# Ten of a step's 36 expert products set among the recurrent gates' products, in the last stage of a two-layer network

## The reference, cut to what matters

```python
def _L1_cond2_ref(video, seq, W_z, U_z, C_z, b_z, W_r, U_r, C_r, b_r, W, U, C, b):
    ...
    def step(h, xs):
        xzt, xrt, xht = xs
        z = jax.nn.sigmoid(xzt + h @ U_z + vz)
        r = jax.nn.sigmoid(xrt + h @ U_r + vr)
        hh = jnp.tanh(xht + r * h @ U + vh)
        h_new = (1.0 - z) * h + z * hh
        return (h_new, h_new)
    ...
def _L1_ffn_ref(x, Wg, routing_bias, W1, W2, W3, Ws1, Ws2, Ws3):
    E, K = (8, 4)
    ...
    h1 = jnp.einsum('bsd,ehd->ebsh', x, W1)
    h2 = jnp.einsum('bsd,ehd->ebsh', x, W2)
    eo = jnp.einsum('ebsh,edh->ebsd', jax.nn.sigmoid(h1) * h1 * h2, W3)
    out = out + jnp.einsum('ebsd,bse->bsd', eo, weights)
    return out
...
x = x + _L1_ffn_ref(_L1_cond2_ref(cond_1024, x, ...), ...)
```

## Time and profile before

| what | value |
|---|---|
| median of 3 runs | 2695.06 us |
| profiled execution, its own time | 2692.25 us |
| span of that execution | 2689.3 us |
| PE busy | 2413.2 us (90%) |
| DVE busy | 1898.1 us (71%) |
| ACT busy | 1206.2 us (45%) |
| steps of chunk 0 (no experts) | from 1573 to 1631 us of the span |
| the 240 steps with both | from 1631 to 2632 us |
| experts of the last chunk alone | from 2632 us to the end |

### The profile page before, as it was taken

How to read it: one execution, slowest core, us unless ns; L and a number is a source line. 1 busy time by engine, 2 the same in 40 slices (tenths; PEclk the granted TensorE clock), 3 DMA queues, 4 the chain that set the end, 5 groups by cost and what they waited for, 6 DMA issues and landing times. The chain is left out here.

```text
span 2689.3 us, 114287 instructions
## 1 busy us (share of the span) xinstructions
PE 2413.2 (90%) x47776; PEld 1955.5 (73%) x47776; DVE 1898.1 (71%) x7976; ACT 1206.2 (45%) x3950; POOL 163.7 (6%) x157
## 2 busy tenths in 40 slices
PE   3778999999999999987758858999999999999999
PEld 2555677777777777754436647888888888888888
DVE  4757777777777777788665666666666666666665
ACT  3225555555555555566436743333333333333333
POOL 0000000000000000000009900000000000000000
PEclk8668999999999999999858968999999999999999
DMA  6000000000000000011003330000000000000000
GB/s 186 2 2 3 5 5 5 5 5 5 5 5 5 6 5 3 5 44 30 4 1 119 95 99 22 9 9 9 9 9 9 9 9 9 9 9 9 5 5 6
DMA packets 53178, 53.35 MB, mean 20 GB/s; under 512 B 25126, under 2 KB 47288, under 8 KB 50746
## 3 DMA queue, kind: packets, MB, share of 16 engines
q1 hardware_dynamic: 47878, 30.57, 4.2%
q0 software_dynamic: 1728, 12.58, 1.4%
q10 hardware_dynamic: 3060, 2.90, 0.4%
HBM read 39.46 MB, written 6.57 MB: 17 GB/s over the span
## 5 line engine op out<-in xcount | busy, mean ns | idle before, releaser
L105 PE MATMUL p<-xn,m_h 128*128 128x128 f16 x6144 | 557.3, 219 | 0.0
L105 PE MATMUL p<-xn,m_l 128*128 128x128 f16 x3072 | 528.6, 219 | 0.0
L105 PEld LDWEIGHTS p<-xn,m_h 128*128 128x128 f16 x6144 | 479.8, 98 | 1.8
L607 PE MATMUL lg_b<-xn,lh 128*32 128x256 f16 x6144 | 300.2, 291 | 77.4 <-DVE lh L1089 69.3
L867 ACT ACTIVATE gl<-gt 128x128 f32<-128x128 f32 x324 | 100.2, 309 | 597.9 <-DVE gt L1065 597.4
L1065 DVE STREAM_TRANSPOSE gt<-lg_b 128x512 f32<-128x512 f32 x324 | 230.0, 710 | 180.5 <-PE lg_b L607 179.9
L882 ACT ACTIVATE hm<-xy,b 128x512 f32<-128x512 f32 x512 | 347.9, 680 | 0.0
L105 PEld LDWEIGHTS p<-xn,m_l 128*128 128x128 f16 x3072 | 300.6, 98 | 0.7
L2038 PE MATMUL po<-m_h,xn 128*128 128x256 f16 x1536 | 292.4, 272 | 2.2 <-DVE xn L2185 1.7
L607 PEld LDWEIGHTS lg_b<-xn,lh 128*32 128x32 f16 x6144 | 159.9, 101 | 161.5 <-DVE lh L1089 117.6
L607 PE MATMUL lg_b<-e_wh_hi,lh 128*32 128x256 f16 x4096 | 209.7, 282 | 30.5 <-DVE lh L1089 29.8
(11 more groups left out here) (400 smaller groups left out, 5975.6 us busy)
## 6 DMA issues: line engine op xcount, KB each, us to landing
m_stage<-in_m_w POOLq DMA_DIRECT2D x12, 1024.0 KB, 5.3
hs<-in_m_w SPq DMA_DIRECT2D x16, 384.0 KB, 3.3
x_dram<-x SPq DMA_DIRECT2D x16, 128.0 KB, 2.1
xs<-in_l_wv SPq DMA_DIRECT2D x1, 2048.0 KB
attention_dram<-att SPq DMA_DIRECT2D x16, 128.0 KB, 3.0
xn<-x_dram SPq DMA_DIRECT2D x16, 128.0 KB, 2.5
xn<-attention_dram SPq DMA_DIRECT2D x128, 16.0 KB, 1.8
out_dram<-xn SPq DMA_DIRECT2D x16, 128.0 KB, 2.2
```

The source lines that it names most:

```text
L105: ins = pe.matmul(out, w[wp](k), x[xp](k), start=start, stop=last and k == KT - 1 and xp == 1, skip_group_check=True)
L607: last = pe.matmul(gate_block(ae, j, par), lh[:, part, ae, k, u, :], columns(w[name], k, j), start=False, stop=(part == 1 and k == KT - 1) ...
```

## The change

TensorE's program of the last stage is put in another order; the instructions are the same. `zr_gates` is cut into `zr_low_weights` and `zr_high_weights`. `hidden` takes a range of its 36 products. In a step with recurrence and experts the first 4 (none in slot 0) stand between the two halves of the gates' products, 26 (30 in slot 0) where all stood, and the last 6 behind the candidate's products, ahead of `down`. The wait for `a_done` stays at the first hidden product, and `hid_pe` is raised by the last one.

```diff
+        HIDDEN, BEFORE, AFTER = 2 * GM * KT * 3, 4, 6
...
-            def zr_gates(i, slot):
+            def zr_low_weights(i, slot):
...
+
+            def zr_high_weights(i, slot):
+                n = i * C + slot
+                par, r = state_at(i, slot)
                 if n > 0:
                     pe.wait_ge(h_lo, n)
...
-            def hidden(i, slot):
+            def hidden(i, slot, lo, hi):
+
                 n = group(i, slot, 0)
-                if n is None:
+                if n is None or lo == hi:
                     return
                 par = (i - 1) % 2
-                if slot == 0:
-                    pe.wait_ge(h_lo, i * C)
-                if n >= 2:
-                    pe.wait_ge(a_done, n - 1)
-                for mat, bank in enumerate((p1[n % 2], p2[n % 2])):
...
+                if lo == 0:
+                    if slot == 0:
+                        pe.wait_ge(h_lo, i * C)
+                    if n >= 2:
+                        pe.wait_ge(a_done, n - 1)
+                banks = p1[n % 2], p2[n % 2]
+                for q in range(lo, hi):
+                    mat, j, k, term = q // 18, q // 6 % GM, q // 3 % KT, q % 3
+                    w, g = (m12_h, m12_l, m12_h)[term], (g_hh, g_hh, g_hl)[term]
+                    last = pe.matmul(banks[mat][:, j * CW:(j + 1) * CW], w[:, mat, k, GM * slot + j, :], g[:, par, k, :],
+                                     start=(q % 18 == 0), stop=(q % 6 == 5), skip_group_check=True)
+                if hi == HIDDEN:
+                    last.then_inc(hid_pe, 1)
...
             for i, slot in steps():
+                before, after = (BEFORE if slot else 0, AFTER) if scans(i) else (0, 0)
                 if scans(i):
-                    zr_gates(i, slot)
+                    zr_low_weights(i, slot)
+                    hidden(i, slot, 0, before)
+                    zr_high_weights(i, slot)
...
-                hidden(i, slot)
+                hidden(i, slot, before, HIDDEN - after)
                 if scans(i):
                     candidate(i, slot)
+                hidden(i, slot, HIDDEN - after, HIDDEN)
```

## The result

The changed kernel takes 2632.26 us, the median of 4 runs (2631.03 to 2633.74). The kernel before, run beside it, takes 2695.05 us. The ratio is 0.9767, with a 95% interval of 0.9742 to 0.9792: faster. Five more runs of the changed kernel, made later beside the last experiments, have a median of 2630.04 us, ratio 0.975 [0.9733, 0.9767].

A forecast was written before the change was run, and what follows sets the result against it. The prediction took TensorE to be full except for two waits on the new state, 0.27 us of each 3.89 us plain step. Gains 52.9 + 2.1 + 3.0 less 1.1 made 56.9 us, giving 2638 us, range 2629 to 2668.

The forecast's parts named there:

- The prediction's two waits: TensorE in each plain step: 0.15 us before the second gate products (`h_lo`), 0.12 before the next step (`h_hi`).
- What it set for being wrong: Plain steps over 3.70 us, line 1983 still waiting for the state, or hidden products starting over 0.06 apart.
- `cand_sum`'s wait: VectorE's wait for the candidate's products in a plain step: to fall from 0.99 to about 0.4 us.
- Slots 6 and 0: Slot 6 should last about 4.40 us instead of 4.32, slot 0 about 4.16 instead of 4.30.
- One sign: Idle time before line 1983's loads left almost only at the start of slot 7, where it grows.
- the plain step: 196 x 0.27 = 52.9: The 196 steps outside slots 0, 1 and 6: each falls from 3.89 to 3.62 us, saving 52.9 together.
- Slots 0 and 1: 15 steps each: slot 0 gains 0.14 us a step, 2.1 in all; slot 1 gains 0.20, 3.0 in all.
- I allow them 0.22: TensorE's first 8 gate products in a plain step: assumed to take 0.22 us, against 0.21 for the second 8.
- its 3.76: Plain step: the state's low half follows 3.76 us after the step's start, asked for at 3.62 + 0.44 = 4.06.
- The first (one wait stays): Rival: the 0.12 us wait before a plain step stays, only the 0.15 goes; 2662 us; chance 0.12.
- The second (short runs cost 0.082 each): Rival: the ten moved TensorE products eat 0.26 of the 0.27 us; near 2693 us, no change; chance 0.06.
- The third (VectorE sets the pace): Rival: `zr_sum` delayed 0.08 us per step and not won back, as in slot 6; slower, 2713 us; chance 0.05.

The follow-up runs named there:

- four and none: Changed kernel with four hidden products between the gates and none behind the candidate instead of six: 2657.89 us, ratio 0.9867.
- Twelve between the gates: Changed kernel with twelve hidden products between the gates instead of four, six still behind the candidate: 2700.45 us, one run, beside 2697.6 for the kernel before.

## Why the prediction was right, and where its sizes were off

The forecast was 2638 us with 2629 to 2668 around it; 2632.26 lies inside, 5.7 below the forecast.

*The mechanism.* The prediction's two waits are gone, as the idle times at lines 1983 and 1993 show. What it set for being wrong did not come: plain steps last 3.59 and not over 3.70, line 1983 does not wait in slot 5 (its step is full), and hidden products start 0.056 apart in the pieces of four and six as in the long run. `cand_sum`'s wait, forecast to fall to about 0.4, is 0.43. Slots 6 and 0, forecast at about 4.40 and 4.16, last 4.37 and 4.125. One sign came half true: idle time before line 1983 was to be left almost only at the start of slot 7, which has 9.4 of the 18.4 us.

*The term that was mis-sized* is the plain step: 196 x 0.27 = 52.9. Added up over the stretch, the plain steps gained 56.6 us, 0.29 each. Slots 0 and 1 gained 2.9 and 3.4 us instead of 2.1 and 3.0, and slot 6 lost 0.7 instead of 1.1. Together this makes the 62.1 of the stretch against the forecast's 56.9. The terms that were too large in the plain step are "I allow them 0.22" for the first 8 gate products, and 0.21 for the second 8. The 0.21 is read from a group that had just waited, and the 0.22 is an allowance next to it. Without a wait both take 0.20, and the plain step is 3.59 instead of 3.62. The runs show it for one and the same order: from line 1983 to line 1993 with four hidden products between, the median is 0.434 us where line 1983 has waited (slot 5 of four and none, and slot 7 of the changed kernel itself) and 0.424 where it has not (slot 5 of the changed kernel). So a group that waits costs its wait and about 0.01 on top, and the prediction counted only the wait.

*What the four are worth.* The prediction gave each part of the change one wait to remove: four for the 0.15, six for the 0.12. The four do fill the first, but they are not needed for it. The six alone remove both waits, because an earlier candidate brings the low half earlier too. The low half is there at 0.20 + 0.20 + 30 x 0.0557 + 1.66 = 3.73, and without the four it is asked for at 3.59 + 0.20 = 3.79. The prediction's own numbers held this, its 3.76 against 3.62 + 0.22 = 3.84. It only asked whether the low half was there with the four. The forecast's sum counts both waits as gone, whichever part removes them, so that its number came near says nothing for this split: on that point the number came near by luck.

*The rivals.* The first (one wait stays) is the size that four and none shows, and not the change. The second (short runs cost 0.082 each) falls: four hidden products take 0.22 and six 0.33 in the rows above, 0.056 each. The rule of the Trainium skill (TensorE: Matmul & The Clock Gate, section Back-to-back issue gap), about 81 ns for a 128-column product in a sustained stream, does not hold here, in pieces no more than in long runs. The third (VectorE sets the pace) is true of slot 6. Twelve between the gates shows that a late `zr_sum` can take the whole gain, but through r * h and the expert's sum.

## What to carry to other kernels

Where a recurrence and independent work share an engine, put the independent work behind the last product that the loop waits for, not ahead of it. The runs show this for one kernel. Work ahead of that product costs its full time in a step that the loop sets (slot 6 grew by 0.22 for four products of 0.22), and nothing where the engine's own work is longer (plain steps, 3.59 with the four and without). Before filling two waits with two pieces of work, see whether the first piece removes both, and ask for each step with a long operation on another engine whether it loses by it. TensorE's busy share of 99% told nothing of 62 us here; the steps read from start to start did.

## What the runs showed that was not expected

- A group of 8 gate products that waited takes about 0.01 us longer to the next kind of product than one that did not: 0.21 from line 1983 to the first hidden product in four and none (2234.54 to 2234.75), and 0.20 in the changed kernel (2219.40 to 2219.60). Why is open.
- The stages ahead of the one that the change touches differ from one execution to the next. Over the ten profiles the last stage's first recurrent step starts between 1566.7 and 1578.7 us, with no edit ahead of it, while the stretch of the changed kernel, profiled twice, differs by 0.3 us. Why is open.
